# Second attention of a fused two-layer block: ScalarE takes over a copy from GpSimd, and four tiles, the key weights and the reciprocals change places

## The reference, cut to what matters

```python
def _L1_xattn_ref(text, features, Wq_w, Wq_b, Wk_w, Wk_b, fn_w, qn_w, kn_w):
    features_n = rmsnorm(features, fn_w)                     # (4, 1601, 512)
    Q = rmsnorm(jnp.einsum('btd,fd->btf', text, Wq_w) + Wq_b, qn_w)         # (4, 256, 512)
    K = rmsnorm(jnp.einsum('bsd,fd->bsf', features_n, Wk_w) + Wk_b, kn_w)
    scores = jnp.einsum('btf,bsf->bts', Q, K) / sqrt(512)
    attn = softmax(scores)
    return jnp.einsum('bts,bsf->btf', attn, features_n)
```

## Time and profile before

| | us |
|---|---|
| median of 3 executions | 3196.44 (3194.53 to 3201.78) |
| profiled execution | 3200.05, of which the span is 3198.3 |
| TensorE busy | 3018.4 (94%) |
| VectorE busy | 2088.2 (65%) |
| ScalarE busy | 1736.0 (54%) |
| GpSimd busy | 945.1 (30%) |

### The profile page before, as it was taken

One profiled execution on the slowest core, in us unless ns is written; L12 is line 12 of the kernel. 1 busy time (PEld: TensorE's weight loads), 2 busy tenths in 40 slices (PEclk: granted clock), 3 DMA queues, 4 the chain that ended last, 5 costly groups with the idle time before them and its releaser, 6 DMA issues. The chain is left out here.

```text
span 3198.3 us, 53821 instructions
## 1 busy us (share of the span) xinstructions
PE 3018.4 (94%) x18397; PEld 2679.7 (84%) x18397; DVE 2088.2 (65%) x3215; ACT 1736.0 (54%) x3299; POOL 945.1 (30%) x773
## 2 busy tenths in 40 slices
PE   8999998999999999999999999979889888999886
PEld 8888887899999999899998999978768778878665
DVE  3333333788888888788887888854443476666576
ACT  3323344676766666666666666632254355545363
POOL 0000121344444444444444444432100044322224
PEclk9999999999999999999999999999989889999899
DMA  7665695776777766677776777557574411100387
GB/s 252 216 216 199 207 289 196 152 160 161 162 163 156 164 157 159 153 161 161 161 159 153 161 160 158 126 158 244 167 264 151 136 42 41 28 26 28 123 300 259
DMA packets 395364, 522.17 MB, mean 163 GB/s; under 512 B 35356, under 2 KB 292684, under 8 KB 395112
## 3 DMA queue, kind: packets, MB, share of 16 engines
q1 hardware_dynamic: 392552, 510.57, 58.6%
q0 software_dynamic: 2560, 8.39, 0.8%
HBM read 238.15 MB, written 146.46 MB: 120 GB/s over the span
## 5 line engine op out<-in xcount | busy, mean ns | idle before, releaser
L707 POOL TENSOR_TENSOR a_t_lo<-a_turned,a_t_hi 128x512 fp32r<-128x512 f32 x512 | 649.2, 1289 | 940.0 <-ACT a_t_hi L836 940.0
L827 ACT ACTIVATE a_probs<-a_ps_s,a_neg_max 128x1024 f32<-128x1024 f32 (+1 forms) x512 | 529.6, 1034 | 475.2 <-DVE a_neg_max L879 472.4
L872 DVE TENSOR_REDUCE a_half_max<-a_ps_s 128x1 f32<-128x1024 f32 (+1 forms) x512 | 571.1, 1116 | 189.3 <-PE a_ps_s L724 185.3
L722 PE MATMUL a_ps_s<-a_k_buf,a_q_buf 128*128 128x512 f32 (+1 forms) x1024 | 419.8, 410 | 17.9 <-ACT a_probs L827 11.5
L723 PE MATMUL a_ps_s<-a_k_buf,a_q_buf 128*128 128x512 f32 (+1 forms) x1024 | 386.2, 377 | 0.0
L724 PE MATMUL a_ps_s<-a_k_buf,a_q_buf 128*128 128x512 f32 (+1 forms) x1024 | 385.2, 376 | 0.0
L908 DVE TENSOR_TENSOR a_x_lo<-a_ps_x,a_x_hi 128x512 fp32r<-128x512 f32 (+1 forms) x512 | 314.4, 614 | 107.7 <-ACT a_x_hi L845 107.7
L454 DVE TENSOR_TENSOR p_out<-p_ps_j,p_out 128x512 fp32r<-128x512 f32 (+3 forms) x196 | 153.1, 781 | 326.8 <-ACT p_out L383 326.8
L898 DVE STREAM_TRANSPOSE a_turned<-xn 128x512 f32<-128x512 f32 x512 | 357.7, 699 | 1.5 <-POOL a_t_lo L707 1.5
L383 ACT ACTIVATE p_out<-p_ps_j 128x512 fp32r<-128x512 f32 (+3 forms) x196 | 142.1, 725 | 339.5 <-PE p_ps_j L288 339.5
L722 PE MATMUL a_ps_o<-a_t_hi,a_v_buf 128*128 128x256 f32 x1024 | 298.8, 292 | 6.4 <-issue 3.9
(11 more groups left out here) (375 smaller groups left out, 7060.4 us busy)
## 6 DMA issues: line engine op xcount, KB each, us to landing
xn<-a_probs SPq DMA_DIRECT2D x1024, 128.0 KB, 3.4
a_q_all<-p_out SPq DMA_DIRECT2D x64, 512.0 KB
a_q_buf<-a_q_all SPq DMA_DIRECT2D x128, 256.0 KB, 3.3
a_k_buf<-a_k_all SPq DMA_DIRECT2D x64, 464.5 KB, 4.0
a_v_all<-p_out SPq DMA_DIRECT2D x56, 512.0 KB
d_w_raw<-e_wt_all SPq DMA_DIRECT2D x31, 768.0 KB, 6.6
a_k_all<-p_out SPq DMA_DIRECT2D x48, 384.0 KB
a_v_buf<-a_v_all SPq DMA_DIRECT2D x64, 256.0 KB
```

Source lines behind the costliest of these rows:

```text
L707: pool.tensor_tensor(t_lo[:, slot, :, :], turned[:, slot, :, :], t_hi[:, slot, :, :].bitcast(F32), ALU.subtract).then_inc(t_done, 1)
L722: pe.matmul(o, w_hi, m_hi, start=first, stop=False)
L827: act.activation(probs[j][u.a][:, lo:hi], s_flat[:, lo:hi], ACT.Exp, bias=neg_max[:, j:j + 1], scale=SCALE, accum_out=half_sum[:, bass.ds( ...
L872: dve.reduce_max(half_max[:, half:half + 1], s_flat[:, lo:hi], AX.X).then_inc(max_done, 1)
```

## The change

1. `f_hi` is written by ScalarE with a copy (`rows_hi`), no longer by GpSimd; GpSimd keeps `f_lo` (`rows_lo`). In the steps ScalarE makes the copies of step s+2 at the very end of step s. The copies of the next batch's tiles 0 to 3 come after the transposed probabilities of the groups (1, 2) and (1, 3), and GpSimd's low parts of them behind those.
2. The transposes of the next batch's tiles 0 and 1 come ahead of the value products (1, 2) and (1, 3). ScalarE's and VectorE's parts of them (`first_features_hi`, `first_features_lo`) end the loop's body, VectorE's ahead of `output(b, 1)`. For batch 0 both are placed ahead of the loop. In the last pass they are made too, for nothing.
3. `key_inverses(s - 1)` at the end of step s becomes `key_inverses(s - 2)` between `features_lo(s + 1)` and the `k_lo` of step s.
4. The query weights get a place of their own (a part of `f_hi` and `f_lo`), and the key weights are transposed and split between the four parts of the last query projection.

```diff
+        wq_hi, wq_lo = f_hi[:, 2 * DC:3 * DC, :], f_lo[:, 2 * DC:3 * DC, :]
 # gpsimd
+            def rows_lo(b, t):
+                n = rows_of(t)
+                pool.wait_ge(f_hi_done, KT * b + t + 1)
+                pool.tensor_tensor(f_lo[0:n, t, :], raw[0:n, t % RING, :], f_hi[0:n, t, :].bitcast(F32),
+                                   ALU.subtract).then_inc(f_done, 1)
+            for t in range(GROUP):
+                rows_lo(0, t)
             with pool.Fori(0, B) as b:
-                for t in range(KT):
...
-                    if t == 0:
-                        pool.wait_ge(o_ps, PRIMED + QT * b)
-                    pool.tensor_tensor(f_hi[0:n, t, :], raw[0:n, t % RING, :], ones[0:n, 0:1].to_broadcast([n, D]),
-                                       ALU.mult).then_inc(f_hi_done, 1)
...
+                for t in range(GROUP, KT):
+                    rows_lo(b, t)
+                for t in range(GROUP):
+                    rows_lo(b + 1, t)
 # tensor
-                    project(f, i % 2, TOK).then_inc(qp_ps, 1)
+                    project(f, i % 2, TOK, wq_hi, wq_lo).then_inc(qp_ps, 1)
+                    if i == B - 1:
+                        transpose_weights(1, f, wk_raw)
...
-            transpose_weights(1, wk_raw)
...
+            def transpose_feature_tile(b, t):
+                n = rows_of(t)
+                pe.wait_ge(f_scaled, KT * b + t + 1)
+                if t >= 2:
+                    pe.wait_ge(ft_done, KT * b + t - 1)
+                else:
+                    pe.wait_ge(pt_done, PRIMED + GROUPS * QT * b - 1 + t)
...
+            for t in TILES_OF[0]:
+                transpose_feature_tile(0, t)
...
-                transpose_features(0)
...
                 for n, (j, g) in enumerate(steps):
                     if 1 < n + 1 < len(steps):
                         transpose_probs(*steps[n + 1])
+                    if n >= len(steps) - 2:
+                        transpose_feature_tile(b + 1, n - len(steps) + 2)
                     weigh(j, g)
 # scalar
+                    if i == B - 1:
+                        weights_hi(DC + f)
...
-            for c in range(DC):
-                weights_hi(DC + c)
+            def first_features_hi(b):
+                for t in TILES_OF[0]:
+                    act.wait_ge(ft_ps, KT * b + t + 1)
+                    if not isinstance(b, int):
+                        act.wait_ge(pv_ps, (GROUPS - 1) * QT * b)
+                    act.activation(t_hi[0][:, :, t * P:(t + 1) * P], by_chunk(ps_t[:, t % 2, :]), ACT.Copy).then_inc(ft_hi_done, 1)
+            def rows_hi(b, t):
+                n = rows_of(t)
+                act.wait_ge(f_scaled, KT * b + t + 1)
+                act.activation(f_hi[0:n, t, :], raw[0:n, t % RING, :], ACT.Copy).then_inc(f_hi_done, 1)
+            first_features_hi(0)
+            for t in range(GROUP):
+                rows_hi(0, t)
...
-                features_hi(0)
...
                         if f == 3 and s:
                             key_roots(s - 1)
+                        if f == 3 and s + 2 < STEPS:
+                            for t in TILES_OF[s + 2]:
+                                rows_hi(b, t)
...
                         if GROUPS * j + g >= 2:
                             probs_hi(j, g)
+                        if j == QT - 1 and g >= 2:
+                            for t in (2 * (g - 2), 2 * (g - 2) + 1):
+                                rows_hi(b + 1, t)
+                first_features_hi(b + 1)
 # vector
+                    if i == B - 1:
+                        weights_lo(DC + f)
...
-            for c in range(DC):
-                weights_lo(DC + c)
...
+            first_features_lo(0)
...
-                features_lo(0)
...
+                    if s >= 2:
+                        key_inverses(s - 2)
                     for f in range(DC):
...
-                    if s:
-                        key_inverses(s - 1)
+                key_inverses(STEPS - 2)
                 key_inverses(STEPS - 1)
...
+                first_features_lo(b + 1)
                 output(b, 1)
```

More of the change, by code:

```diff
@@ L1462, in normed_attention_block @@
     widths = [max(n for s, (_, n) in enumerate(COLS) if s % 2 == a) for a in range(2)]
-    assert len(CHUNKS) == 4 and D == BANK and QT == 2 and GROUPS == 4 and LAST < P and KT % 2 == 1 and STEPS % 2 == 0
+    assert len(CHUNKS) == 4 and D == BANK and QT == 2 and GROUPS == 4 and GROUP == 4 and RING == 4 and LAST < P and KT % 2 == 1 and STEPS % 2 == 0
     with ExitStack() as ctx:
@@ L1575, in three, with transpose_weights, project @@
                 return pe.matmul(out, a_lo, m_hi, start=False, stop=last)
-            def transpose_weights(which, tiles):
-                pe.wait_ge(*((wk_loaded, 16 * DC) if which else (wq_loaded, 16)))
-                for c in range(DC):
[L1580 to L1589, removed]
-                for c in range(DC):
-                    mm = three(ps_s[:, f, 0:n], w_hi[:, c, f * P:(f + 1) * P], w_lo[:, c, f * P:(f + 1) * P],
+            def transpose_weights(which, c, tiles):
+                n = DC * which + c
+                if c == 0:
+                    pe.wait_ge(*((wk_loaded, 16 * DC) if which else (wq_loaded, 16)))
+                if n >= 2:
+                    pe.wait_ge(w_done, n - 1)
+                if which:
+                    pe.wait_ge(xt_done, TILES)
+                for t in range(DC):
+                    tr = pe.transpose(ps_t[:, n % 2, t * P:(t + 1) * P], tiles[t][:, c * P:(c + 1) * P], ident[:, :])
+                tr.then_inc(w_ps, 1)
+            def project(f, a, n, hi=w_hi, lo=w_lo):
+                for c in range(DC):
+                    mm = three(ps_s[:, f, 0:n], hi[:, c, f * P:(f + 1) * P], lo[:, c, f * P:(f + 1) * P],
                                t_hi[a][:, c, 0:n], t_lo[a][:, c, 0:n], c == 0, c == DC - 1)
@@ L1612, in sum_query_squares @@
                 mm.then_inc(qs_ps, 1)
-            transpose_weights(0, [raw[:, t, :] for t in range(DC)])
+            for c in range(DC):
+                transpose_weights(0, c, [raw[:, t, :] for t in range(DC)])
             pe.wait_ge(rows_loaded, 96)
@@ L1633, in _ @@
             pe.wait_ge(q_root, 1)
+            def transpose_feature_tile(b, t):
[5 more added lines that the diff above has]
+                    pe.wait_ge(pt_done, PRIMED + GROUPS * QT * b - 1 + t)
+                for c in range(DC):
+                    tr = pe.transpose(ps_t[:, t % 2, c * P:c * P + n], raw[0:n, t % RING, c * P:(c + 1) * P], ident[0:n, 0:n])
+                tr.then_inc(ft_ps, 1)
+            for t in TILES_OF[0]:
+                transpose_feature_tile(0, t)
             with pe.Fori(0, B) as b:
@@ L1731, in weights_hi @@
                 act.wait_ge(w_ps, n + 1)
[L1732 to L1735 removed]
+                act.activation((wq_hi if n < DC else w_hi)[:, n % DC, :], ps_t[:, n % 2, :], ACT.Copy,
                                scale=1.0 if n < DC else columns[:, FN, n % DC:n % DC + 1]).then_inc(w_hi_done, 1)
@@ L1901, in _, with first_features_lo @@
             scale_tiles(1, 0)
-            for c in range(DC):
-                weights_lo(DC + c)
             dve.wait_ge(q_inv_done, 1)
+            def first_features_lo(b):
+                for t in TILES_OF[0]:
+                    dve.wait_ge(ft_hi_done, KT * b + t + 1)
+                    dve.tensor_tensor(t_lo[0][:, :, t * P:(t + 1) * P], by_chunk(ps_t[:, t % 2, :]),
+                                      t_hi[0][:, :, t * P:(t + 1) * P].bitcast(F32), ALU.subtract).then_inc(ft_done, 1)
+            first_features_lo(0)
             with dve.Fori(0, B) as b:
```

20 lines of the change are left out of this document (2 added, 18 removed).

## The result

The changed kernel takes 3165.12 us (median of 4, 3163.82 to 3167.02) against 3196.56 for the kernel before in the same comparison (4, 3194.53 to 3201.78): ratio 0.9896 [0.9881, 0.9912], 31.4 us less. The forecast was 3168.0 in 3156 to 3184. The profiled execution took 3163.82, its span is 3162.1.

The account below looks back on a forecast made before the run. TensorE's waits, 39.0 us and nearly all for VectorE, were taken to bound the second attention. Terms -5.3 - 14.5 - 6 - 5 + 1.8 = -29, called -28, from the median 3196.44 gave 3168 us, range 3156 to 3184.

Parts of the forecast that it names:

- ahead of the loop: Last query sum to first key matmul: interleaving the key weights makes 14.8 us into 9.5, -5.3 (bounds -3.5 to -7).
- waits in the steps: TensorE's waits in the second attention's steps fall from 24.5 to 10 us over four batches, -14.5.
- handovers: Between batches, TensorE's gap of 2.37 us shrinks to about 0.4, -2.0 three times, -6.
- clock: Slow TensorE stretches behind handovers and tile 10's waits, 6 us in all: 5 given back, bounds 0 and 6.
- the end, the last pass: Idle transposes (+1.0) and VectorE's two idle low parts (0.8) in the last pass: +1.8, bounds 1.0 to 2.5.
- first rival: Steps: GpSimd's hold-up of VectorE stays, only the reciprocal's 1.74 and a microsecond elsewhere go per batch; 3180 us, chance 0.18.
- the two weak bounds: Smallest gains allowed ahead of the loop (-3.5) and at each handover (-1.5), said to turn -23 into -16.
- a sign of being wrong: In the steps: VectorE's second addition, L1952, still above 1 us in most steps would show the forecast wrong.
- lateness of 0.4, 1.1 and 1.6: ScalarE late by these microseconds at its first parts of steps 1, 2 and 3, since copies stand ahead of `features_hi`.
- slower rival: Steps: ScalarE stalls at the copies; a copy of 1.3 us would eat the gain of 28; 3205 us, chance 0.05.

Follow-up runs that it names:

- key weights: Changed kernel with the key weights' transposes and splits behind the query sums again: 3169.75 us, ratio 0.9906 to the kernel before.
- reciprocals: Changed kernel with step s-1's reciprocals back at the end of step s: 3179.14 us, ratio 0.9930 to the kernel before.
- high parts: Changed kernel with the features' high parts on GpSimd again, directly ahead of each low part: 3176.08 us, ratio 0.9925 to the kernel before.
- the undoings: Four runs of the changed kernel, each with one part of the change taken back: ratios 0.9930, 0.9906, 0.9925 and 0.9920 to the kernel before.
- the second profile of the changed kernel: The changed kernel, nothing altered, measured and profiled again on another chip: ratio 0.9895 to the kernel before, loop 359.76 us.
- tiles 0 and 1 back at the loop's head: Changed kernel with transposes and splits of each batch's tiles 0 and 1 at the loop's head again: 3175.32 us, ratio 0.9920.
- short low parts: Changed kernel with GpSimd's low parts of tiles 4 to 12 computed for 32 of 512 columns only: 3165.52 us, ratio 0.9891.
- doubled copies: Changed kernel with each ScalarE copy in the steps made twice, the second into scratch, nine more per batch: 3187.82 us, ratio 0.9965.
- reciprocals alone: Kernel before the change with only the reciprocals moved as in the change: 3185.91 us, ratio 0.9960.
- copies later: Changed kernel with ScalarE's copies moved behind `features_hi` at the head of the next step: 3172.61 us, ratio 0.9918 to the kernel before.

## Why the prediction was right

By its own terms, forecast against the profile:

| term | forecast | profile | undone |
|---|---|---|---|
| ahead of the loop | -5.3 | -5.8 | +4.4 (key weights) |
| waits in the steps | -14.5 | -13.9 | +8.5 (reciprocals), +7.3 (high parts) |
| handovers | -6 | -6.3 | +5.9 |
| clock | -5 | -8.8 | in the rows above |
| the end, the last pass | +1.8 | +1.7 | |

The third column is read from the two profiles, the fourth from the windows of the undoings; it holds waits and clock together. By the second profile of the changed kernel the waits in the steps are -15.6 and the clock -7.2: the two trade about 1.6 us between executions while the loop stays the same.

*Ahead of the loop.* The layout by hand gave 7.4 us behind the sums; 7.21 were measured. The price of the weights' transposes between the query parts was put at 2.1; from the start of the head the sums end 1.7 later (44.4 us for 42.7), 0.8 in the second profile.
*Waits in the steps.* 24.5 fell to 10.6 (9.1 and 1.5), forecast 10; in batch 1 step 5 starts 37.1 us after step 0, where the layout had 37.2. Tile 10's was below 1.5 as foretold. The scaled tiles' were to stay under 1 each; five of them didn't, step 4's in every batch (1.05 to 1.23) and one of 1.31 in batch 0.
*Handovers.* 2.37 to 0.28, forecast 0.4. The mechanism, ScalarE's high part behind product (1, 2) and the output behind both low parts, is in the timeline.
*The clock.* This is the term that was mis-sized. The slow stretches were counted rightly, five, but put at 1.0 to 1.6 us each, 6 in all, of which I gave back 5. Each withheld 1.7, 8.5 in all, and none is left; my bound was 6. No window of batches 1 to 3 is under 1.00 now.
*The end.* VectorE's two low parts hold the last output for 0.7, and the next stage's transposes got 0.7 back as they came at the higher clock earlier, which I hadn't seen. What is left of the loop when waits and clock are taken off grew by 1.7; most of it (1.2) goes with tiles 0 and 1 back at the loop's head. That it is the last pass's transposes, put at 1.0, is argued.

So the sum came out 3 to 5 us short of what was measured, most of it in the clock.

**A step that held by half** is the reason I gave for part of the steps' term: "part of the hold-ups, as GpSimd has one instruction per tile instead of two". Its worth is shown: with two instructions per tile again the loop is 7.3 us longer, the waits 6.3. With the reciprocals' 6.7 that is 13.0 of the 13.9. The first rival, in which only the reciprocal and a microsecond elsewhere go, put the steps at -10.8 and the time at 3180, and it is out. (Its -16 doesn't follow from the two weak bounds named with it, which make -19.5; it needs the clock's 2.5 at nothing and the end at its worst too.) But its mechanism is there for the second addition. GpSimd's low part starts when ScalarE's copy ends, just when the additions run: L1991 is down to 0.73 us in the mean, while L1993, the old L1952, went from 1.10 to 1.21, and of all that VectorE lost in the loop (10.7 us) the additions make only 3.2. That L1952 would stay above 1 us I had named as a sign of being wrong; it came, and the term held all the same, because the second instruction had also held the first addition and the scaling of tile 12. What the second addition's hold-up still costs is at most the 4.3 us of the short low parts.

In the trace the two stand together: the second addition starts at 2677.10 and takes 1.40, while GpSimd, from 2676.91, takes 2.75 for two low parts, so that the first ends about when the addition does; freed, the addition takes 0.43. The Trainium skill (SBUF — State Buffer, who interferes with whom) says that a VectorE instruction with two SBUF inputs is blocked for the length of a GpSimd instruction that reads SBUF, if that one issued first, and the trace agrees. The length of the hold-up is not its price: here 16.6 us of held VectorE were at most 4.3 of the loop.

**ScalarE** was judged the tight engine with lateness of 0.4, 1.1 and 1.6, and the copy at 0.52 between starts is exact. The doubled copies bear that out: of 18.7 us more of its work 14.8 to 16.5 show as TensorE's waits. The loop grew by more, 21.1, since longer waits brought the lower clock back (6.9). So the slower rival's conversion, a microsecond per copy as a microsecond of time, was about right in its sum, by two parts that it didn't have, and its condition, a copy of 1.3, did not come.

## What to carry to other kernels

A long instruction in an in-order queue is moved behind the short one for which the critical engine waits, before any work is made faster: the reciprocals alone brought over a third of the gain and cost nothing. A hold-up between two engines is priced by taking it away, not by its length: a quarter of it at most was on the path. The waits of TensorE and what its lower clock withholds are read apart: longer waits can cost twice, by their length and by the clock behind them, and a loop can lose 5 us with hardly longer waits in all. Before an instruction on a full engine is put later, follow what hangs on it to the end, buffers and reloads included; an edit that costs time alone can gain some beside another that removes the wait it creates.

## What the runs showed of the hardware

With the copies later a pause of 1.93 us of TensorE in the steps was followed by transposes at lower speed (1.76 for eight against 1.09); so the clock fell behind three of its four pauses of that kind (1.93, 2.04 and 1.96), and not behind the fourth (1.92). In the changed kernel's batches 1 to 3, with pauses of 0.2 to 1.23, the granted clock stays at 1.00. In the kernel with the reciprocals back four pauses of about 2.0, one in each batch, had the clock fall in one batch only, and in the kernel before the 3.09 of batch 1 was followed by matmuls at full pace (0.28), where the 2.37 of the first handover wasn't (0.41). So the length of the pause alone doesn't decide it. What else does was not tried.
